# A two-layer graph network kernel: the first norm's low halves computed on GpSimd during the second sort, and the norm ended on ScalarE before that sort's counts

## The reference, cut to what matters

```python
edge_index = jnp.stack([src, dst])
h = jnp.maximum(_layernorm(x, axis=-1), 0.0)
x = x + _L0_gnn_ref(h, src, dst, L0_gnn_W, L0_gnn_b)      # segment_sum(h[src], dst) @ W.T + b
h = jnp.maximum(_layernorm(x, axis=-1), 0.0)
x = x + _L1_gnn_ref(h, edge_index, ...)                   # 12 steps: agg by edges / degree, MLP, tanh, update
return x
```

## Time and profile before

| what | value |
|---|---|
| device time, median of 3 runs | 1405.81 us (1405.77 to 1406.26) |
| the profiled execution's own time | 1406.44 us |
| its span, first to last instruction | 1404.7 us |
| mean granted TensorE clock | 0.963 of full speed |

### The profile page before, as it was taken

The page is one execution under the profiler, slowest core; times in us unless marked ns, Lnnn a source line. Parts: engine busy times, 40 slices in busy tenths (PEclk is TensorE's granted clock), DMA queues, the critical chain, the costliest instruction groups (busy, mean ns, idle before and its releaser), DMA issues.

```text
span 1404.7 us, 21715 instructions
## 1 busy us (share of the span) xinstructions
PE 1269.6 (90%) x9386; PEld 741.4 (53%) x9386; DVE 905.0 (64%) x1298; ACT 325.2 (23%) x698; POOL 7.9 (1%) x18
## 2 busy tenths in 40 slices
PE   3766567789999999999999999999999999999995
PEld 2633555555555555555555555555555555555553
DVE  8999999955455465655646655465664556655464
ACT  0500348835521111211111111111111111111111
POOL 2000000000000000000000000000000000000000
PEclk9688869999999999999999999999999999999997
DMA  3000000021100000000000000000000000000100
GB/s 113 2 1 8 2 1 1 2 73 40 35 1 1 1 0 1 1 1 1 0 1 1 1 1 1 1 1 1 0 1 1 1 1 1 1 1 1 47 22 25
DMA packets 11917, 13.95 MB, mean 10 GB/s; under 512 B 1997, under 2 KB 10414, under 8 KB 11438
## 3 DMA queue, kind: packets, MB, share of 16 engines
q1 hardware_dynamic: 10484, 11.98, 2.7%
q10 hardware_dynamic: 1338, 0.59, 0.2%
HBM read 7.67 MB, written 4.89 MB: 9 GB/s over the span
## 4 chain that ended last, share of the span: by engine, by line
PE 59%; DVE 15%; issue 2%; ACT 2%; DVEq 0%
PE psum L829 46%; PE psum L887 7%; PE psum L877 5%; DVE work L1163 3%; DVE work L1160 2%; DVE work L1175 2%; DVE state L1177 2%; DVE work L1168 2%; ACT work L1016 1%; DVE parts L1184 1%; DVE agg L1144 1%; DVE work L1150 1%; DVE work L1148 1%; PE psum L841 0%; PE psum L856 0%
## 5 line engine op out<-in xcount | busy, mean ns | idle before, releaser
L829 PE MATMUL psum<-adj,parts 128*128 128x512 f16 (+2 forms) x4550 | 891.6, 352 | 3.7 <-PEq L648 2.1
L829 PEld LDWEIGHTS psum<-adj,parts 128*128 128x128 f16 x4550 | 441.4, 98 | 398.6 <-issue 2.5
L1144 DVE TENSOR_TENSOR agg<-psum,rdeg 128x512 f32<-128x512 f32 (+2 forms) x84 | 52.3, 622 | 217.7 <-PE psum L829 216.4
L1016 ACT ACTIVATE work<-work 128x512 f32<-128x512 f32 (+1 forms) x84 | 49.0, 584 | 597.5 <-DVE work L1168 597.5
L1011 ACT ACTIVATE work<-psum,b_col,gelu_scale 128x512 f32<-128x512 f32 (+2 forms) x168 | 112.1, 717 | 248.0 <-PE psum L877 248.0
L887 PE MATMUL psum<-w_half,work 128*128 128x128 f16 x1800 | 115.3, 220 | 16.1 <-DVE work L1163 15.3
L887 PEld LDWEIGHTS psum<-w_half,work 128*128 128x128 f16 x1800 | 106.3, 98 | 40.5 <-issue 29.1
L1163 DVE SCALAR_TENSOR_TENSOR work<-work,mlp_scale 128x512 f16<-128x512 f32 (+2 forms) x168 | 115.0, 684 | 6.0
L1160 DVE TENSOR_SCALAR work<-work,mlp_scale 128x512 f16<-128x512 f32 (+2 forms) x168 | 75.2, 447 | 59.0 <-PE psum L887 38.9
L877 PE MATMUL psum<-work,w_half 128*128 128x512 f16 (+2 forms) x504 | 109.3, 353 | 2.1 <-DVE work L1150 1.8
L1175 DVE SCALAR_TENSOR_TENSOR work<-state,decay,work 128x512 f32<-128x512 f32 (+1 forms) x84 | 58.3, 694 | 54.7 <-ACT work L1016 54.7
(11 more groups left out here) (158 smaller groups left out, 698.7 us busy)
## 6 DMA issues: line engine op xcount, KB each, us to landing
x_scratch<-parts SPq DMA_DIRECT2D x1, 1600.0 KB, 5.2
parts<-x_scratch SPq DMA_DIRECT2D x1, 1600.0 KB, 6.6
rdeg<-rdeg_scratch SPq DMA_DIRECT2D x1, 1568.0 KB, 7.5
work<-x_scratch SPq DMA_DIRECT2D x4, 256.0 KB, 2.6
x_scratch<-work SPq DMA_DIRECT2D x4, 256.0 KB, 2.0
work<-x_scratch SPq DMA_DIRECT2D x3, 192.0 KB, 2.6
x_scratch<-work SPq DMA_DIRECT2D x3, 192.0 KB, 1.9
state<-in_L_gnn_W SPq DMA_DIRECT2D x2, 128.0 KB, 2.0
```

The lines of the kernel that those rows point to most:

```text
L829: last = nc.tensor.matmul(bank_of(n)[:, 0:width(c)], parts[:, at:at + D], adj[:, k * NP + cols(c).start:k * NP + cols(c).stop], start=(k = ...
```

## The change

Two things move. On ScalarE the 25 ReLUs and the rounding copy now stand ahead of `copy_base` and `copy_rank` of the second sort. The subtraction leaves VectorE; GpSimd makes it, as its first work after the fills, when `s_hi0` is raised. VectorE's wait for `s_lo0` moves from tile 0 of the tile loop to tile 1, the first that writes over `x_all`.

```diff
                 pool.memset(all_ones, 1.0).then_inc(s_zero, 1)
+                pool.wait_ge(s_hi0, 1)
+                nc.gpsimd.tensor_tensor(ln_parts[:, :, 1, :], x_all, ln_parts[:, :, 0, :], ALU.subtract).then_inc(s_lo0, 1)
...
-                copy_base(BASE2, PAIR2, CLASSES, v2[0], q_base, q_basec)
-                for g in range(len(RANK2)):
-                    copy_rank(RANK2, g, U2, rank2, q_rank, q_rankc)
                 act.wait_ge(s_inv0, 1)
                 act.wait_ge(s_xkept, 16)
                 for k in range(KT):
...
                 nc.scalar.activation(ln_parts[:, :, 0, :], x_all, ACT.Copy).then_inc(s_hi0, 1)
+                copy_base(BASE2, PAIR2, CLASSES, v2[0], q_base, q_basec)
+                for g in range(len(RANK2)):
+                    copy_rank(RANK2, g, U2, rank2, q_rank, q_rankc)
...
                 nc.vector.tensor_copy(overflow[:, :], ps[FLAGB][:, 0:1]).then_inc(s_flagc, 1)
-                dve.wait_ge(s_hi0, 1)
-                nc.vector.tensor_tensor(ln_parts[:, :, 1, :], x_all, ln_parts[:, :, 0, :], ALU.subtract).then_inc(s_lo0, 1)
-                dve.wait_ge(s_lo0, 1)
                 dve.wait_ge(q_tabc, 2 * len(TAB2))
                 for k in range(KT):
                     wait(dve, s_mused, (k - 1) * J)
                     row = slice(k * CLASSES, (k + 1) * CLASSES)
+                    if k == 1:
+                        dve.wait_ge(s_lo0, 1)
```

## The result

| | before | changed |
|---|---|---|
| device time, median of 9 runs each | 1405.78 us (1404.81 to 1407.81) | 1410.23 us (1409.79 to 1413.08) |
| the profiled execution and its span | 1406.44, 1404.7 us | 1410.41, 1408.7 us |

The changed kernel is slower: the ratio is 1.0033, with a 95% interval from 1.0024 to 1.0042. By the medians that is 4.45 us, by the two profiled executions 3.97 us.

A forecast was written before the change was run, and what follows sets the result against it. VectorE was taken to set the end while the matrix is built. A hold of +7.3 us less a 1.6 us gain gave +5.7 us: 1411.5 us from a 1405.81 us median, range 1403.7 to 1413.7 us.

The forecast's parts named there:

- What bounds the kernel: While the matrix is built, VectorE sets the end: busy 23.00 of 23.00 us from 88, 97.73 of 102.00 in the loop.
- the gain of the removal: Without VectorE's subtraction the tile loop starts at about 186.33 instead of 187.96 us, bounded by ScalarE's table copies: 1.6 us.
- the 0.5 us allowed for the clock: Margin either way on the 1.6 us gain, for TensorE's clock level at the start of the tile loop.
- ScalarE's move at no cost: ReLUs and rounding run from 72.70 to about 85.3 us, 4.5 us ahead of the second sort's count copies at 89.80.
- The hold: At the seam at 87.65 us GpSimd's subtraction gets in and VectorE stands 7.3 us ahead of L422; chance 0.55.
- No hold: Rival: GpSimd works beside VectorE, done by about 93 us; only the gain is left, 1404.2 us; chance 0.27.
- a partial hold: Rival: engines take turns inside instructions, VectorE loses 1.5 to 5.8 us; 1405.7 to 1410.0 us; chance 0.10.
- the late start: Rival: GpSimd waits for a real VectorE pause, ahead of 142.41 or behind 181.31 us; 1408.8 to 1410.2 us; chance 0.08.
- 25 masks of 0.29 us: Length of GpSimd's subtraction, from its shortest 128-column mask row: 7.3 us, with 11.5 us as upper bound.
- L401 beside the iota: Sign for a hold: VectorE's first instruction took 1.11 us, its twin L412 0.38, with GpSimd in its iota; 0.73 us lost.
- The L408 row: Sign against a hold: two VectorE instructions overlapping a GpSimd fill took 5.64 us, as the same size did without company.
- The estimate from the Trainium skill: GpSimd's subtraction length from the page's 4497 ns for an f32 addition of 2048 columns: 7.0 us.

The follow-up runs named there:

- the first run: Changed kernel with the subtraction back on VectorE, so only ScalarE's ReLUs and rounding stand earlier; 1406.15 us, ratio to before 1.000.
- the second profiles: Both kernels profiled once more, unchanged, one run each: 1406.35 us for before, 1413.34 us for the changed kernel.
- the half-size run: Changed kernel with GpSimd subtracting only tiles 0 to 12 of 25 and VectorE the rest behind the flag; 1408.38 us, ratio 1.0016.
- the run with GpSimd second: Changed kernel with GpSimd's subtraction released by the end of the first value product, the second product already running; 1410.02 us (one run).
- the fills beside copies: Changed kernel with three GpSimd fills in place of the subtraction and four idle VectorE f32 copies ahead of the value products; 1418.38 us (one run).
- fills against copies on GpSimd: Changed kernel, VectorE subtracting behind the flag: GpSimd makes three fills (1405.79 us) or three copies of x_all (1412.9 us), one run each.

## Why the prediction was right, point by point

- **What bounds the kernel, and the gain of the removal: right.** VectorE sets the end in this stretch: its 5.92 us at the flag's reduce are the 5.93 us of the products. The gain was put at 1.6 us because the tables end last; it is 1.65 us, with the loop's start released by the tables (`[1.78 <-ACT rdeg L386]`). Too small was the 0.5 us allowed for the clock: it moved the flag's copy by 0.97 us one way and the end of the loop's first pause by 0.68 us the other, and that the two nearly cancel in the profiled execution is luck. The first section needs a word too: the engines do not meet only at semaphores; VectorE waited 5.94 us for GpSimd with no semaphore between them.
- **ScalarE's move at no cost: right,** shown alone in the first run. One detail was off: the copies of counts came at 91.35, not 89.80, behind TensorE's counts (granted clock 0.93 from 88 to 111 us in the changed kernel, 0.99 in the earlier trace rows); the last of them still ended before the products. This belongs to the execution: in the second profiles they came at 91.39 in before and at 89.81 us in the changed kernel.
- **The hold: right in kind, place and duration rule.** GpSimd came into the last one-hots, waited for their end, got in at the seam and held the first product for its whole length. The prediction gave this 0.55. No hold has the row of 11.72 us against it, a partial hold the half-size run, in which the whole length is added, and the late start the run with GpSimd second.
- **Its size: the term that was off.** The prediction put 25 masks of 0.29 us, 7.3 us; the hold is 5.93 us. The half-size run gives (5.93 - 3.03) / 12 = 0.24 us for a tile of 128 columns, so the mask's row was the right neighbour and 0.05 us too long. With 5.93 in its place the sum is +4.3 us, or 1410.1 us, against 1410.23 measured; the forecast of 1411.5 missed by the length of this one term. (In the chances, half of the partial hold's 0.10 is 0.05, not 0.04; nothing hangs on it.)
- **The evidence was weaker than its weight.** L401 beside the iota was read as a sign that a subtraction would hold a two-input product. The runs show two different cases: a fast one-input copy is held even by GpSimd work that only writes (the fills beside copies), a two-input product only by GpSimd work that reads (fills against copies on GpSimd). L401 has one input and ended 0.23 us behind the iota (6.36 against 6.13 us), about what 416 columns take at the copy's 0.57 ns, so it looks like the first case; that it was the engine's first instruction stays possible. The L408 row rightly said that writes alone hold no two-input instruction. Neither row could have shown the case at hand: as far as these rows go, that the hold came true was luck.

The rule that the prediction set beside them named the case. By the Trainium skill (SBUF — State Buffer, Who interferes with whom), two SBUF inputs contend with a GpSimd instruction that reads, one input outside the two-port modes does not, copies in those modes do, and whoever comes second waits for the whole of the other. All runs here agree with it: held for 6.07 us (2.6 by a GpSimd copy) in the first case, 0 in the second, 5.95 in the third. That the f32 copy ran in such a mode no row shows by itself; its 0.57 ns an element against the reduce's 1.09 fits. The estimate from the Trainium skill (GPSIMD Engine Reference, Elementwise — side-by-side cycle accounting), 7.0 us by its f32 figure, was too long: 6.07 us were measured, for f32 less f16 to f16.

That the shortest mask was the nearest row is luck as well. It was taken because the other two ran beside VectorE's work, but so did this one, which the earlier trace rows has from 6.87 to 7.16 us. VectorE's timeline of before at that time:

```profile
6.39 0.59 DVE L402 SCALAR_TENSOR_TENSOR state<-state 128x416 f32<-128x416 int32 x1
...
7.02 0.38 DVE L403 TENSOR_SCALAR state<-state 128x416 f32<-128x416 f32 x1
```

What stays open: why executions place TensorE's change of clock level on either side of the sort's end (over the two profiles of each kernel it moved the flag's copy by 1 us without any change in the code), and which property of the copy makes it wait where the reduce does not.

## What to carry to other kernels

An idle GpSimd is not a free engine: before work that reads SBUF is handed to it, look at what VectorE runs at that time. Beside the two-input products, one-hots and the f32 copy it took VectorE's time one for one, here at 1.7 times the price that VectorE itself asked (5.93 against 3.48 us); beside reduces, or when it only wrote and VectorE's work had two inputs, it was free. And before work is moved to another engine, look for a pause on its own: the subtraction fitted into a pause 2 us earlier in the same queue.

A held instruction did not show as idle time. It showed as one row longer than its twins, so compare minimum, median and maximum of a line, not its sum.

## What the runs showed of the hardware that was not expected

- A VectorE queue without gaps did not starve GpSimd: it got in at the next instruction boundary and the third product of four back-to-back ones paid 6.07 us.
- With instructions waiting on both sides the two engines alternated one by one: copies of 2.6 us and products of 5.78 us gave rows of 8.30 and 8.43 us on either side.
- Three fills of 2.77 us left two-input products untouched, and a fast one-input copy of 1.81 us beside the same fills grew to 4.46 us: what GpSimd does is not enough to tell whether VectorE is held; the kind of VectorE's instruction decided.
